# A mixture-of-experts layer: one TensorE signal for two steps of the shared expert, and the last batch's routing three steps sooner

## The chip, the core and the metric

The kernel runs on one core of a Trainium2 chip. The metric is the device time of one execution in microseconds (us), the median over several runs.

## The reference, cut to what matters

The input x has 8 batches of 512 rows of 128 numbers. An attention layer with 16 heads, a residual and a layer norm give x1. After it comes a mixture of experts: a gate picks two of eight experts for each row, and one shared expert takes every row.

```python
gates = sigmoid(xf @ Wg)
vals, idx = top_k(gates, 2); vals = vals / vals.sum(-1, keepdims=True)
shared = (silu(xf @ Ws1) * (xf @ Ws3)) @ Ws2
h = silu(einsum('td,edf->tef', xf, We1)) * einsum('td,edf->tef', xf, We3)
routed = einsum('tef,efd,te->td', h, We2, w)   # w: the two weights of each row, else 0
out = layernorm(x1 + (shared + routed) / 3)
```

## The kernel before

Every engine has its own program; they meet at semaphores only. There are three stages.

**Attention** runs quad by quad (four quads a batch, 32 in all) and works the routing of a batch into the attention of later ones. The routing of the last batch is left over, and parts of the last but one.

**The shared expert** has 32 steps, `n = 4 * b + c`: four for each batch b. Step (b, c) makes one 128 x 512 piece of the hidden layer, by three matmuls (lines 1477 to 1479) into bank c of `hT`. Even c is the half that goes through silu, odd c the half that it is multiplied with. So a pair of steps is worked off thus:

- ScalarE applies silu to the even bank (line 1367, `siluT_done`).
- VectorE multiplies it with the odd bank (line 1274, `gatedT_done`).
- TensorE may fill the pair's two banks again, one batch later, when that product is there (line 1475).

TensorE increments `hT_ready` after each step; ScalarE waits for `n + 1` at even n, VectorE at odd n.

Beside the steps run, in this order within a batch:

- At c = 0 TensorE turns the next batch's x1 (`turn_x`, line 679). ScalarE rounds it at c = 1 (`x_high`, line 686), VectorE takes the rest at c = 2 (`x_low`, line 691). Step (b + 1, 0) waits for both.
- At c = 1, 2, 3 TensorE does the second layer of the batch before (`shared_results`, line 1459), two tiles, one and one. It signals `ys_ready` after the last. Its first tiles wait for both products of that batch and for `sum_done`, which says that the results of the batch before that have been read out of the one bank they share.
- At c = 0 VectorE reads out those results, two batches back (`add_shared`, line 1262), in the order of its program: after the product of step (b, 3) and what stands beside that step.

What stands beside a step is written out by hand, by the step's number (`beside`, in TensorE's program for jobs, in VectorE's for routing). VectorE does the remaining routing of the last but one batch at steps 0 to 8, and that of the last at 9 to 25:

- `choose` pieces 0 to 7 at steps 9 to 16, one a step, each some two or three small instructions. They find each row's two experts.
- TensorE counts rows per expert (`count_rows`, at `COUNT_AT` = 16, after piece 6); VectorE reads the counts at step 17.
- `place` pieces 0 to 4 at steps 18 to 22. Piece 3 ends with `slot_i` (line 458), the slot of each row.
- The block owners at step 23, turned by TensorE at `OWNER_AT` = 24, read at 25 (`routed`).

When `slot_i` is there, GpSimd scatters the rows into their slots in DRAM by eight indirect DMAs (line 488). When they have all landed, SP's queue loads the blocks of 128 rows (line 1206).

**The routed experts**: TensorE does the last batch's `shared_results` (16 recorded matmuls), waits for `routed` and for the blocks and begins with 72 blocks (lines 1490, 1509 to 1532). For each, an indirect DMA from GpSimd writes the result to its rows (line 1178). Sums and the last layer norm run beside it.

Of the kernel before, what the change touches and what calls it, by code (L numbers as in the profile page):

```python
# [104 lines left out]
def layer(nc, x, w_qkv, b_qkv, w_out, b_out, wg, ws1, ws3, ws2, we1, we3, we2, out):  # L105
    B, S, D = x.shape
# [25 lines left out]
    with ctx:  # L132
        def sb(name, shape, dt=F32):
            return ctx.enter_context(nc.sbuf_tensor(name, shape, dt))
# [30 lines left out]
        ebT_low = sb("ebT_low", [P, 2, 512], F32R)  # L165
# [121 lines left out]
        def need(eng, s, value):  # L287

            if isinstance(value, int) and value <= 0:
                return  # L290
            eng.wait_ge(s, value)
            if not isinstance(value, int) and eng.engine in ALONE:


                eng.sem_inc(passed, 1)
# [374 lines left out]
        hT_ready = sem("hT_ready")  # L670
# [11 lines left out]
        def x_high(act, b):  # L682

            act.wait_ge(xT_ready, b + 1)
            need(act, hT_ready, 4 * (b - 1))
            act.activation(ebT_high[:, b % 2, :], xT_bank, ACT.Copy).then_inc(xT_high_done, 1)

        def x_low(dve, b):
# [378 lines left out]


        BESIDE = {0: ("counts", "valsT"), 1: ("oT",), 2: ("proj",), 7: ("x1T",), 8: ("gate",)}
        COUNT_AT, OWNER_AT = 16, 24  # L1070
        STAGE_OF = {"counts": 1, "valsT": 1, "oT": 1, "proj": 2, "x1T": 3, "gate": 3}

        early = prob[:, 0].rearrange("p h c t -> p (h c t)")
# [69 lines left out]
        hT = scoreA[:].rearrange("p a b x -> p (a b) x")  # L1143
# [71 lines left out]
        def moe_vector(dve):  # L1215
            def beside(n):

                if n == 0:
                    read_counts_job(dve, B)
                    dve_job(dve, "valsT", B, 1)  # L1220
                elif n in (1, 2):
                    place(dve, B - 2, n - 1)
                elif n == 3:
                    dve_job(dve, "proj", B, 2)
                    statistics(dve, B, 1)
                elif n == 4:
                    statistics(dve, B, 3)
                    statistics(dve, B, 5)
                elif n == 5:
                    place(dve, B - 2, 2)  # L1230
                elif n == 6:
                    normalize(dve, B, 1)
                    normalize(dve, B, 3)
                elif n in (7, 8):
                    place(dve, B - 2, n - 4)
                elif n == 9:
                    dve.wait_ge(job_read, jobs.number("gate", B, 3) + 1)
                    choose(dve, B - 1, 0)
                elif n in range(10, 17):
                    choose(dve, B - 1, n - 9)  # L1240
                elif n == 17:
                    dve.wait_ge(counts_ready, 1)
                    read_counts(dve, B - 1, shared, counts_read)
                    dve.wait_ge(counts_read, 1)
                elif n in range(18, 23):
                    place(dve, B - 1, n - 18)
                elif n == OWNER_AT - 1:

                    dve.wait_ge(late_const, 4)
                    dve.scalar_tensor_tensor(passed_ends[:], all_ends[:], block_no[:, 0:1], turn[:], ALU.is_le,  # L1250
                                             ALU.mult).then_inc(owner_done, 1)
                    dve.wait_ge(owner_done, 1)
                    dve.tensor_reduce(owner[:], passed_ends[:].rearrange("p b e -> p (b e)"), AX.X, ALU.add) \
                       .then_inc(owner_done, 1)
                elif n == OWNER_AT + 1:
                    dve.wait_ge(owner_ready, 1)
                    dve.tensor_copy(owner_i[0:1, :], late_owner).then_inc(routed, 1)
# [7 lines left out]
            for n in range(STEPS):  # L1265
                b, c = n // 4, n % 4
                if c == 0 and b >= 2:
                    add_shared(b - 2)
                if c % 2:

                    need(dve, ys_ready, b - 1)
                    dve.wait_ge(siluT_done, 2 * b + c // 2 + 1)
                    dve.wait_ge(hT_ready, n + 1)
                    dve.tensor_tensor(gatedT_shared[:, b % 2, c // 2, :], hT[:, c], silu_shared[:, c // 2, :],
                                      ALU.mult).then_inc(gatedT_done, 1)
                if c == 2 and b + 1 < B:
                    x_low(dve, b + 1)
                beside(n)
# [81 lines left out]
        def moe_scalar(act):  # L1360
            for n in range(STEPS):
                b, c = n // 4, n % 4
                if c % 2 == 0:
                    act.wait_ge(hT_ready, n + 1)

                    need(act, gatedT_done, 2 * (b - 1) + c // 2 + 1)
                    act.activation(silu_shared[:, c // 2, :], hT[:, c], ACT.Silu).then_inc(siluT_done, 1)
                if c == 1 and b + 1 < B:
                    x_high(act, b + 1)
                for kind in BESIDE.get(n, ()):  # L1370
                    if kind in ("oT", "x1T", "gate"):
                        act_job(act, kind, B, STAGE_OF[kind])

            def ebT_highs(r, n):
                act.wait_ge(ebT_ready, n + 1)
                need(act, h_ready, n - 1)
                act.activation(ebT_high[:, r % 2, 0:P], scoreA[:, 1, r % 2, 0:P], ACT.Copy).then_inc(ebT_high_done, 1)  # L1377

            ebT_highs(0, 0)
            ebT_highs(1, 1)  # L1380

            def final_normalize(batch, c):
                need(act, fmr_done, batch.n + 1)
                at = z[:, batch.slot, c, :]
                act.activation(at, at, ACT.Identity, scale=frs[:, c:c + 1], bias=fmr[:, c:c + 1]).then_inc(norm_done, 1)

            def store_out(batch):

                need(act, norm_done, 4 * (batch.n + 1))
                act.dma_start(out_rows[batch.n] if isinstance(batch.n, int) else  # L1390
                              out_rows[bass.ds(batch.n, 1)].rearrange("b p x -> (b p) x"),
                              z[:, batch.slot].rearrange("p c d -> p (c d)")).then_inc(out_stored[batch.slot], 16)

            NORMALIZED_AT = {4: (0,), 5: (1,), 6: (2, 3)}

            def block(g, r):
                k = g.k
                n = NBUF * k + r
                if exists(k, r):
                    act.wait_ge(h_ready, n + 1)  # L1400
                    need(act, gated_done, n - 1)
                    act.activation(silu[:, r % 2, :], scoreA[:, 0, r % 2, 0:F], ACT.Silu).then_inc(silu_done, 1)  # L1402
                if exists(k, r, 2):
                    c = (r - 2) % NBUF
                    at = NBUF * ((g.odd + (r - 2) // NBUF) % 2) + c
                    act.wait_ge(y_ready, n - 1)

                    need(act, y_stored[c], 16 * (k if r >= 2 else k - 1))
                    act.activation(yo[:, c, :], scoreB[:, r % 2, 0:D], ACT.Copy,  # L1409
                                   scale=eb[:, at, D + 1:D + 2]).then_inc(y_done, 1)  # L1410
                if exists(k, r, -2):
                    ebT_highs(r + 2, n + 2)
                if ended(g, 4):
                    for c in NORMALIZED_AT.get(r, ()):
                        final_normalize(ended(g, 4), c)
                    if r == NBUF - 1:
                        store_out(ended(g, 4))

            run_blocks(act, block)

        def moe_tensor(pe):
# [45 lines left out]
            for n in range(STEPS):  # L1467
                b, c = n // 4, n % 4

                at = E * 2 * F + (c % 2) * F + (c // 2) * P  # L1470
                high, low = (w[:, at:at + P] for w in w13_parts)
                if c == 0:
                    pe.wait_ge(xT_low_done, b + 1)

                need(pe, gatedT_done, 2 * (b - 1) + c // 2 + 1)

                pe.matmul(hT[:, c], high, ebT_high[:, b % 2, :], start=True, stop=False)
                pe.matmul(hT[:, c], low, ebT_high[:, b % 2, :], start=False, stop=False)
                pe.matmul(hT[:, c], high, ebT_low[:, b % 2, :], start=False, stop=True).then_inc(hT_ready, 1)
                if c == 0 and b + 1 < B:  # L1480
                    turn_x(pe, b + 1)
                if c and b:
                    shared_results(b - 1, ((0, 1), (2,), (3,))[c - 1])
                beside(n)
# [105 lines left out]
```

## Time and profile before, and how to read it

| what | us |
|---|---|
| time, median of 3 runs (lowest, highest) | 695.01 (694.5, 696.32) |
| span of the profiled execution | 737.1 |
| the profiled execution: TensorE busy | 656.4 |
| the profiled execution: VectorE busy | 551.6 |
| the profiled execution: ScalarE busy | 425.3 |
| the profiled execution: GpSimd busy | 269.0 |

The profiled execution is one that ran with the profiler on. Its span, from the first to the last instruction, is 42.1 us longer than the median time of the runs without it. Nothing else of that execution's time is recorded. Durations below are from it.

PE is TensorE, PEld its weight loads, DVE VectorE, ACT ScalarE, POOL GpSimd, SP SyncE, and a q behind a name that engine's queue or sequencer. L1479 is line 1479. A row's start is in us from the span's start; a number in brackets is how long the engine was idle before, and whom it waited for. Ends of matmuls are modelled, and an instruction of VectorE or ScalarE can begin before the row of the one before has ended. Tiles of the shared stage lie in the attention's `prob`, so many rows bear that name.

### The profile page before, as it was taken

To read this page: it belongs to the slowest core of one execution; us is meant where nothing else is said; L and a number is where in the kernel's file an instruction comes from. 1 tells how busy PE (TensorE), PEld (TensorE's weight loads), DVE (VectorE), ACT (ScalarE), POOL (GpSimd) and SP (SyncE) were. 2 spreads that over 40 slices of the span, in tenths; PEclk is the share of its full clock that TensorE was granted. 3 is DMA by queue.
4 is the path that set the end of the run, shared out by engine and by line. 5 is a ranking of instruction groups with operands and counts; after the bars stand their busy time and mean duration, and the time that the engine had idled before them with its cause. 6 is when DMAs were issued, how large, how long until landed. Compare 5 with 4: busy or idle time off the path is not lost.

```text
span 737.1 us, 16627 instructions
## 1 busy us (share of the span) xinstructions
PE 656.4 (89%) x4593; PEld 318.7 (43%) x4594; DVE 551.6 (75%) x1272; ACT 425.3 (58%) x973; POOL 269.0 (36%) x402
## 2 busy tenths in 40 slices
PE   2899999999899999999999999987988888888880
PEld 1232333333333343433433333322777766666660
DVE  4967777879779989998997997964756556666663
ACT  1056677677576677677676776673522344455442
POOL 3124114213154145134334334124144345555553
PEclk9999999999999999999999999998989999999885
DMA  4356766544234324333333333203111323433222
GB/s 79 75 130 153 145 136 120 110 89 92 57 66 97 82 61 91 70 80 79 71 76 84 74 55 85 53 24 113 38 44 40 78 76 99 123 113 110 89 71 71
DMA packets 161855, 62.65 MB, mean 85 GB/s; under 512 B 110586, under 2 KB 155516, under 8 KB 161808
## 3 DMA queue, kind: packets, MB, share of 16 engines
q1 hardware_dynamic: 155008, 46.72, 29.4%
q0 software_dynamic: 5648, 13.26, 6.0%
q10 hardware_dynamic: 1152, 2.10, 0.8%
q8 instruction: 23, 0.38, 0.2%
q14 instruction: 24, 0.20, 0.1%
HBM read 38.04 MB, written 24.26 MB: 85 GB/s over the span
## 4 chain that ended last, share of the span: by engine, by line
PE 76%; DVE 5%; issue 5%; ACT 4%; DMA 4%; another core or an unknown queue 2%; SPq 1%; POOL 1%; ACTq 0%; DVEq 0%; POOLq 0%
PE pvp L1018 16%; PE scoreB L998 15%; PE scoreA L984 14%; PE scoreB L1532 6%; PE scoreA L1509 3%; ACT prob L901 2%; PE scoreA L1511 2%; PE pvp L1519 2%; PE shared L525 2%; DMA parts_dram<-parts 2%; PE scoreA L1510 2%; DVE mx L928 2%; PE scoreB L1459 2%; PE shared L514 2%
## 5 line engine op out<-in xcount | busy, mean ns | idle before, releaser
L928 DVE TENSOR_REDUCE mx<-scoreA 128x2 f32<-128x1024 f32 x256 | 305.9, 1220 | 70.7 <-PE scoreA L984 68.3
L901 ACT ACTIVATE prob<-scoreB 128x512 f32<-128x512 f32 x512 | 279.5, 600 | 120.3 <-PE scoreB L998 117.9
L984 PE MATMUL scoreA<-ks,qs 72*128 72x512 bf16 x512 | 205.5, 409 | 14.8 <-DMA ks<-parts_dram 12.4
L998 PE MATMUL scoreB<-qs,ks 74*128 74x512 bf16 x512 | 200.5, 394 | 9.9 <-ACT prob L901 6.7
L1018 PE MATMUL pvp<-prob,v 128*32 128x512 f32 x1024 | 139.0, 616 | 0.8 <-ACT pv_sb L893 0.8
L984 PEld LDWEIGHTS scoreA<-ks,qs 72*128 72x128 bf16 x512 | 51.0, 102 | 155.6 <-DVE mx L928 66.7
L1178 POOL DMA_INDIRECT y_dram<-prob x72 | 70.7, 982 | 75.7 <-ACT prob L1409 50.5
L998 PEld LDWEIGHTS scoreB<-qs,ks 74*128 74x128 bf16 x512 | 49.8, 99 | 103.8 <-ACT prob L901 78.9
L488 POOL DMA_INDIRECT slots_dram<-rows,slot_i x64 | 63.3, 990 | 62.9 <-DMA ks<-parts_dram 31.2
L828 POOL CAST parts<-qk 128x256 bf16<-128x256 f32 x32 | 12.7, 397 | 187.2 <-ACT v_raw L563 168.4
L1409 ACT ACTIVATE prob<-scoreB,prob 128x128 f32<-128x128 f32 x72 | 26.5, 369 | 42.2 <-PE scoreB L1532 35.0
L1348 DVE TENSOR_TENSOR prob<-scoreA,prob 128x256 f32<-128x256 f32 x72 | 30.5, 423 | 22.5 <-ACT prob L1402 14.9
L1532 PE MATMUL scoreB<-w,prob 128*128 x288 | 47.3, 290 | 0.0
L1509 PE MATMUL scoreA<-w_high,ebT_high 128*128 x72 | 36.5, 508 | 11.1 <-DVE ebT_low L1283 6.8
L1402 ACT ACTIVATE prob<-scoreA 128x256 f32<-128x256 f32 x72 | 27.6, 384 | 29.6 <-PE scoreA L1511 19.8
L1283 DVE TENSOR_TENSOR ebT_low<-scoreA,ebT_high 128x128 fp32r<-128x128 f32 x72 | 20.7, 289 | 27.5 <-ACT ebT_high L1377 18.5
L1532 PEld LDWEIGHTS scoreB<-w,prob 128*128 128x128 f32 x288 | 40.5, 203 | 0.2
L1519 PE MATMUL pvp<-ident,prob 128*128 128x128 f32 x144 | 29.8, 290 | 10.9 <-DVE prob L1353 9.7
L1018 PEld LDWEIGHTS pvp<-prob,v 128*32 128x32 f32 x1024 | 20.5, 109 | 31.0 <-issue 29.5
L1353 DVE COPY prob<-pvp 128x256 f32<-128x256 f32 x72 | 29.9, 415 | 1.8 <-PE pvp L1519 1.8
L559 ACT ACTIVATE qk<-shared,bq 128x128 f32<-128x128 f32 x64 | 20.0, 363 | 18.4 <-PE shared L514 12.7
L1519 PEld LDWEIGHTS pvp<-ident,prob 128*128 128x128 f32 x144 | 16.7, 146 | 30.0 <-issue 16.0
(172 smaller groups left out, 886.5 us busy)
## 6 DMA issues: line engine op xcount, KB each, us to landing
qs<-parts_dram SPq DMA_DIRECT2D x96, 96.0 KB
parts_dram<-parts SPq DMA_DIRECT2D x32, 192.0 KB
slots_dram<-blank POOLq DMA_DIRECT2D x9, 520.0 KB
prob<-slots_dram SPq DMA_DIRECT2D x72, 65.0 KB
ks<-parts_dram SPq DMA_DIRECT2D x64, 64.0 KB
prob<-y_dram SPq DMA_DIRECT2D x8, 512.0 KB
ks<-parts_dram SPq DMA_DIRECT2D x32, 96.0 KB
xin<-in_L_attn_x SPq DMA_DIRECT2D x32, 64.0 KB, 2.3
```

The costliest lines, as they stand in the source:

```text
L488: pool.indirect_dma_start(slots_dram, bass.IndirectOffsetOnAxis(ap=slot_i[:, j, t:t + 1], axis=0), rows[:, t, j, :], None).then_inc(scatte ...
L901: act.activation(prob[:, i % 2, j, 2 * u + c, :], scoreB[:, c], ACT.Exp, scale=SCALE).then_inc(exp_done, 1)
L928: dve.tensor_reduce(mx[:, i % 2, at // 2, at % 2 * 2:at % 2 * 2 + 2], scoreA[:, at % 2], AX.X, ALU.max).then_inc(max_done, 1)
L984: ins = pe.matmul(scoreA[:, at % 2, c], qs[0:KR, st, j, qc * P:(qc + 1) * P], ks[0:KR, st, j, :], start=True, stop=True)
L998: pe.matmul(scoreB[:, c], ks[0:KM, i, j, kc * P:(kc + 1) * P], qs[0:KM, i, j, :], start=True, stop=True).then_inc(b_ready, 1)
L1018: ins = pe.matmul(pvp[32 * h:32 * h + 32, :], v[:, (i - 1) % 2, h, j, :], prob[:, (i - 1) % 2, h, j, :], start=(j == 0), stop=(j == 3))
L1178: pool.indirect_dma_start(y2_dram, bass.IndirectOffsetOnAxis(ap=eb[:, at, D:D + 1].bitcast(I32), axis=0), yo[:, r, :], None, bounds_check= ...
L1348: dve.tensor_tensor(gated[:, r % 2, :], scoreA[:, 0, r % 2, F:2 * F], silu[:, r % 2, :], ALU.mult) \
L1353: dve.tensor_copy(gatedT[:, (r - 1) % 2, :], pvp[:, 0:F]).then_inc(gT_copied, 1)
L1509: pe.matmul(h, ebT_high[:, r % 2, 0:P], high, start=True, stop=False)
L1519: ins = pe.transpose(pvp[:, c * P:(c + 1) * P], gated[:, (r - 1) % 2, c * P:(c + 1) * P], ident[:])
L1532: ins = pe.matmul(y, gatedT[:, r % 2, c * P:(c + 1) * P], w2_flat[:, bass.ds(e * NFC * D + c * D, D)], start=(c == 0), stop=(c == NFC - 1))
```

## The change

Four things change.

- TensorE increments `hT_ready` at odd c only. ScalarE's silu of an even step and VectorE's product wait for `n // 2 + 1`, so both for the end of the pair's odd step. `x_high`'s bound is halved to match.
- VectorE's choice for the last batch goes two pieces a step: 0 and 1 at step 9, then 2 and 3, 4 and 5, 6 and 7 at steps 10 to 12.
- The counts go from step 16 to 13 (read at 14 instead of 17), the five pieces of `place` from 18 to 22 to 15 to 19.
- The owners go from steps 23, 24 and 25 to 20, 21 and 22.

```diff
-            need(act, hT_ready, 4 * (b - 1))
+            need(act, hT_ready, 2 * (b - 1))
...
-        COUNT_AT, OWNER_AT = 16, 24
+        COUNT_AT, OWNER_AT = 13, 21
...
                 elif n == 9:
                     dve.wait_ge(job_read, jobs.number("gate", B, 3) + 1)
                     choose(dve, B - 1, 0)
-                elif n in range(10, 17):
-                    choose(dve, B - 1, n - 9)
-                elif n == 17:
+                    choose(dve, B - 1, 1)
+                elif n in range(10, 13):
+                    choose(dve, B - 1, 2 * (n - 9))
+                    choose(dve, B - 1, 2 * (n - 9) + 1)
+                elif n == 14:
                     dve.wait_ge(counts_ready, 1)
                     read_counts(dve, B - 1, shared, counts_read)
                     dve.wait_ge(counts_read, 1)
-                elif n in range(18, 23):
-                    place(dve, B - 1, n - 18)
+                elif n in range(15, 20):
+                    place(dve, B - 1, n - 15)
...
-                    dve.wait_ge(hT_ready, n + 1)
+                    dve.wait_ge(hT_ready, n // 2 + 1)
...
-                    act.wait_ge(hT_ready, n + 1)
+                    act.wait_ge(hT_ready, n // 2 + 1)
...
-                pe.matmul(hT[:, c], high, ebT_low[:, b % 2, :], start=False, stop=True).then_inc(hT_ready, 1)
+                ins = pe.matmul(hT[:, c], high, ebT_low[:, b % 2, :], start=False, stop=True)
+                if c % 2:
+                    ins.then_inc(hT_ready, 1)
```

## Rows read from the trace of the kernel before

**Rows 1.** The page: the chain that ended last, and one group of DMAs.

```profile
PE 76%; DVE 5%; issue 5%; ACT 4%; DMA 4%; another core or an unknown queue 2%; SPq 1%; POOL 1%; ACTq 0%; DVEq 0%; POOLq 0%
...
xin<-in_L_attn_x SPq DMA_DIRECT2D x32, 64.0 KB, 2.3
```

**Rows 2.** TensorE's groups, 517 to 575 us: busy us, mean ns, idle us before.

```profile
L1459 PE MATMUL scoreB<-w,prob 128*128 128x128 f32 x128 | 19.0, 286 | 2.7 <-DVE prob L1262 2.7
L1477 PE MATMUL scoreA<-ebT_high,w_high 128*128 128x512 f32 x32 | 15.7, 491 | 2.5 <-DVE prob L1274 2.5
...
L538 PE MATMUL shared<-ident,x 128*128 128x128 f32 x4 | 0.6, 279 | 0.7 <-DVE x L628 0.7
```

**Rows 3.** The chain that ended last, 530 to 640 us: start, us, what.

```profile
544.60 0.61 ACT prob L1367
545.28 0.69 DVE prob L1274
...
552.94 0.23 PE scoreA L1479
...
554.31 0.44 PE scoreB L679 x4
...
555.45 0.89 PE scoreB L1459 x8
```

**Rows 4.** VectorE in stretches holding one piece each: stretch, us, busy, clock, DMA.

```profile
534.24:534.88 0.64, 0.58 (x3) 1.00 0.33 104
...
543.07:543.38 0.31, 0.28 (x3) 1.00 0.00 0
543.99:544.40 0.41, 0.37 (x3) 1.00 0.00 0
550.71:551.67 0.96, 0.89 (x7) 0.50 0.00 0
532.16:532.80 0.64, 0.61 (x7) 1.00 0.39 102
```

**Rows 5.** Timeline of VectorE, around step 19.

```profile
553.31 0.69 DVE L1274 TENSOR_TENSOR prob<-scoreA,prob 128x512 f32<-128x512 f32 x1 [1.64 <-PE scoreA L1479]
553.92 0.17 DVE L426 TENSOR_TENSOR_SCAN ends<-ones,more 128x8 f32<-128x8 f32 x1
```

**Rows 6.** Timeline of VectorE, the product of step 3.

```profile
524.60 0.69 DVE L1274 TENSOR_TENSOR prob<-scoreA,prob 128x512 f32<-128x512 f32 x1 [0.59 <-PE scoreA L1479]
```

**Rows 7.** Timeline from the slots to the end of the shared stage.

```profile
557.15 0.17 DVE L458 CAST slot_i<-slot 128x8 int32<-128x8 f32 x1
...
568.85 8.66 SPq L1206 DMA_DIRECT2D prob<-slots_dram  x16
...
569.69 0.40 PE L1479 MATMUL scoreA<-ebT_low,w_high 128*128 128x512 f32 x1
...
570.22 0.69 DVE L1274 TENSOR_TENSOR prob<-scoreA,prob 128x512 f32<-128x512 f32 x1 [0.27 <-PE scoreA L1479]
...
571.66 2.02 PE L1459 MATMUL scoreB<-w,prob 128*128 128x128 f32 x16 [1.13 <-DVE prob L1262]
```

**Rows 8.** Timeline of steps 13 to 16, while GpSimd issues indirect DMAs.

```profile
538.09 0.40 PE L1479 MATMUL scoreA<-ebT_low,w_high 128*128 128x512 f32 x1
...
542.47 0.69 DVE L1274 TENSOR_TENSOR prob<-scoreA,prob 128x512 f32<-128x512 f32 x1 [4.10 <-PE scoreA L1479]
...
544.13 0.50 PE L1477 MATMUL scoreA<-ebT_high,w_high 128*128 128x512 f32 x1 [2.48 <-DVE prob L1274]
```

**Rows 9.** Stretches of 10 us: engines' busy us, granted clock, DMA share, GB/s.

```profile
540.00:550.00 10.00, 6.80 (x33) 5.64 (x32) 4.78 (x16) 2.33 (x4) 3.75 (x7) 0.76 0.07 22
550.00:560.00 10.00, 9.76 (x57) 8.30 (x56) 7.94 (x36) 2.93 (x6) 2.02 (x2) 0.90 0.02 7
```

**Rows 10.** L1509 (one a block) in two stretches of the routed stage.

```profile
577.02:580.08 3.06, 0.96 (x2) 0.39 (x3) 1.00 0.34 75
585.47:591.02 5.55, 1.44 (x3) 0.56 (x3) 1.00 0.23 66
```

## The prediction, made before the changed kernel was run

> **What bounds the kernel now.** I read the chain that ended last first: TensorE carries 76% of the span and VectorE 5% [rows 1]. So a change beside TensorE counts only where TensorE waits for it. Next, TensorE's groups over the shared stage, the only stage the change touches: it waits 2.7 us before the second layer, for `add_shared`; 2.5 us before a step's first matmul, for a product; and 0.7 us before x1's transposes [rows 2]. Everything else there runs without idle time. In particular no idle time is booked between a signalling matmul and the next instruction, so dropping sixteen increments frees no time on TensorE itself. Then the timelines, for the distance between a step's end and each of those waits; and last the stretches, for clock and lateness (below).
>
> **One signal for two steps: what a product costs in time.** Before, silu of the even step ran while TensorE was still in the odd step, and the product began 0.14 us after the odd step's end: step 19 ended at 552.94 + 0.23 = 553.17, its product began at 553.31 [rows 3, 5]; for step 31 it is 570.09 and 570.22 [rows 7]. Now silu itself waits for the odd step. From the odd step's end: 0.03 us to ScalarE (an estimate, somewhat under VectorE's 0.14), silu 0.60, and 0.07 from silu to product (544.60 + 0.61 to 545.28) [rows 3]. Together 0.70 us, so every product comes 0.56 us later. That is certain, 16 times; what matters is where TensorE has less slack than that.
>
> The bound is the chain from step (b, 3) through `add_shared` to the second layer at step (b + 1, 1). VectorE is held 0.61 us by the product (553.31 to 553.92) [rows 5], then does what stands beside the step (call it p), then `add_shared`, 0.68 us like the other 512-wide operations, and TensorE follows 0.15 us after it (the second layer at 571.66, when an `add_shared` started as soon as the product of 570.22 let go) [rows 7]. Before: 0.14 + 0.61 + 0.68 + 0.15 = 1.58 + p. After: 2.14 + p. TensorE gets there 2.28 us after the step's end (553.17 to 555.45) [rows 3], as step, turn, step and the last second-layer tiles lie between. So before there was 0.70 us of room for p; after there is 0.14, and the rest of p is idle time on TensorE. This is where the two halves of the change meet: the doubled choice makes p larger just when the room goes.
>
> Term by term, with pieces from [rows 4]:
> - Step 11: p is choice pieces 4 and 5, 0.31 + 0.41 = 0.72 us (before, one piece). Wait 0.58. VectorE is also behind: from the product of step 9 it does 0.61, pieces 0 and 1 (0.64 + some 0.4), x_low 0.6 and pieces 2 and 3 (some 0.8), 3.05 us, starting 0.70 after step 9's end. It is free at 3.75; the product of step 11 is due 2.73 (0.89 + 0.70 + 0.44 + 0.70) + 0.70 = 3.43 after that end. 0.3 more: **0.9**.
> - Step 15: p is `place` piece 0, 0.96: **0.8**.
> - Step 19: p is piece 4, 0.64: **0.5**.
> - Step 27: p is 0, but the last batch has no turn in between (0.44 less [rows 3]): 1.84 against 2.14, **0.3**.
> - Step 31: TensorE waits 1.13 us before the last second layer already [rows 7], so the later product is paid in full: **0.55**.
> - The first batches: x1's transposes wait for a VectorE that has no pause from step 1's product to the normalize but 0.59 us before step 3's [rows 6]. Step 1's product slips 0.56, step 3's by that again, less the pause, plus TensorE's own slip through the attention output's later copy on ScalarE (which now stands behind a later silu). Bounds 0.55 and 1.2; taken **1.0**.
>
> Sum 4.05, taken as 4.0 us. If all slips were hidden it would be 0; with the upper bound at each place (each p with its semaphore gaps, 0.1 to 0.2 more) 5.5.
>
> **Counts, placing, owners three steps sooner.** Same instructions, none added; their room beside the steps is counted in p. On TensorE the count and the owners' transpose only change place: nothing, or up to 0.7 us less if a wait of the count for the choice goes. The slots are ready three steps sooner, some 3 to 4 us. GpSimd has nothing queued before the scatter by then and SP nothing but the block loads, so both start sooner. What is that worth? From `slot_i` at 557.15 eight scatters run until SP issues the first load at 568.85; with the 2.3 us that a 64 KB load takes to land [rows 1] block 0 is there at about 571.2, while TensorE is busy until 573.68 [rows 7]. So the blocks are 2.5 us early already, and earlier still buys nothing. If TensorE's two late waits are taken out (below), it arrives at about 571.3, a tie: still nothing. The cover for the later start is gone only if TensorE came faster.
>
> **Late signals.** One thing in the trace speaks for the change. Step 13 ended at 538.49, yet its product began at 542.47, VectorE idle for 4.1 us, and TensorE then stood 2.48 us [rows 8] and fell to 1.2 GHz for parts of the next stretches (clock 0.76 and 0.90) [rows 9]. ScalarE's silu at 544.60 [rows 3] is as late. This happens only while GpSimd issues indirect DMAs. It happens in the routed stage too: blocks come every 1.53 us at first, then every 1.85 us [rows 10], 0.32 us x 72 = 23 us. With fewer signals, fewer could be late.
>
> How does the profiled execution stand to the runs? It is 42.1 us longer than the median. The 23 us, some 7.5 us in the shared stage (2.48, 1.6 of the 2.7, and 3.4 for the clock: 0.24 and 0.10 of 10 us) and the clock's loss in the routed stage make up most of those 42. So I take it that timed runs have few late signals, and the sum of 4.0 holds for them: 695.0 + 4.0 = **699.0 us** (the profiled execution: 737.1 to 741).
>
> **Rivals.**
> 1. *Late signals are real in timed runs; the halved number ends them.* TensorE sends four instead of six signals a batch (two pairs, the turn, the second layer). All 7.5 us back, less the 4.0: 3.5 us faster, 691.5. It decides for faster once over 6.1 us of 7.5 come back. For: [rows 8, 9]. Against: the 42 us, and that a pair's signal can be late as well, with less room behind it. The Trainium skill, "VectorE: DVE Perf Modes", section on the TRN2 errata, warns that dense increments on completion from several engines should be spaced; by that rule this change is the remedy and the time would go down; the trace agrees that signals arrive late, not why. Chance 0.13.
> 2. *The routing's tail binds in timed runs.* If scatter and load take 2 to 4 us longer without the profiler's company than [rows 7] show, or late signals cost half of theirs, what the earlier slots return cancels the later products: 694.5 to 697. For: the tie above. Against: nothing shows such a load. Chance 0.2.
> 3. *The slips are hidden.* If ScalarE and VectorE hand over faster than in the rows, 0.56 shrinks and the room of 0.14 grows; only the end's 0.55 and part of the first batch remain, 696. This goes into rival 2's chance.
>
> The forecast, slower by 2.1 to 6 us, has 0.67. 0.3% of 695 us is 2.1 us, about what a measurement of this kernel can tell from no change. Faster 0.13, same 0.2, slower 0.67. The range reaches down through the same case and up to 5.5 us and a little, for a lost clock: 694.3 to 701.0. The forecast's own range is 697.2 to 701.0.
>
> **What would show it.** Right: silu of each even step starts after the odd L1479's end; TensorE's idle time before L1459 grows from 2.7 us, spread over steps 13, 17, 21 and 29, and that before L538 from 0.7 to about 1.7; L458 comes some 14 us or more before TensorE reaches L1490, which waits for no block. Wrong: no idle time before L1459 outside the last one; or, for rival 1, products that begin within 0.2 us of silu all through the scatters, with the clock at full between; or L1490 waiting for blocks in the old kernel.

## The result, and the profile after

The changed kernel takes 702.88 us (median of 6 runs, 700.99 to 706.49), the kernel before in the same session 694.75 us (6 runs, 691.88 to 696.32): ratio 1.0133, 95% interval 1.0105 to 1.016. A second timing gave 1.0106, 1.007 to 1.0143. So it is slower, by some 8 us; 4 were forecast, in a range up to 701.0 us. The profiled execution took 703.39 us, with a span of 701.6.

The profile of before that the prediction read was of an unusual execution: its span of 737.1 us and its late signals [rows 8, 10] came back in none of the later profiles. A second profile of the unchanged kernel has a span of 694.0 us, in a run of 695.73. It is called **before 2** here, and everything below is measured against it.

TensorE's groups from 505 to 575 us: busy us, mean ns, idle us before them. First before 2, the undisturbed form of [rows 2]:

```profile
L1459 PE MATMUL scoreB<-w,prob 128*128 128x128 f32 x128 | 18.0, 276 | 1.2 <-DVE prob L1262 1.1
L1477 PE MATMUL scoreA<-ebT_high,w_high 128*128 128x512 f32 x32 | 15.1, 472 | 0.0
...
L538 PE MATMUL shared<-ident,x 128*128 128x128 f32 x4 | 0.6, 280 | 0.7 <-DVE x L628 0.7
```

Then the changed kernel, whose lines here lie two further on (L1461 is L1459, L1479 is L1477, L1264 is L1262; L538 and L691 are unmoved):

```profile
L1461 PE MATMUL scoreB<-w,prob 128*128 128x128 f32 x128 | 18.3, 278 | 4.1 <-DVE prob L1264 4.1
L1479 PE MATMUL scoreA<-ebT_high,w_high 128*128 128x512 f32 x32 | 15.2, 474 | 2.4 <-DVE ebT_low L691 2.4
...
L538 PE MATMUL shared<-ident,x 128*128 128x128 f32 x4 | 0.6, 279 | 1.2 <-DVE x L628 1.2
```

Three things can be read off. The wait before the second layer grew by 2.9 us, about as the prediction said, and the one before x1's transposes (L538) by 0.5, half of what it said. But a step's first matmul, which waited for nothing, now waits 2.4 us, and not for a product: for `x_low` (L691). No term of the prediction stands for that.

The timeline of TensorE in the changed kernel gives the places:

```profile
526.64 0.63 PE L538 MATMUL shared<-ident,x 128*128 128x128 f32 x4 [1.21 <-DVE x L628]
...
533.84 0.50 PE L1479 MATMUL scoreA<-ebT_high,w_high 128*128 128x512 f32 x1 [0.68 <-DVE ebT_low L691]
...
536.82 1.13 PE L1461 MATMUL scoreB<-w,prob 128*128 128x128 f32 x8 [0.89 <-DVE prob L1264]
...
542.41 0.51 PE L1479 MATMUL scoreA<-ebT_high,w_high 128*128 128x512 f32 x1 [1.74 <-DVE ebT_low L691]
...
545.03 1.13 PE L1461 MATMUL scoreB<-w,prob 128*128 128x128 f32 x8 [0.51 <-DVE prob L1264]
...
550.91 1.13 PE L1461 MATMUL scoreB<-w,prob 128*128 128x128 f32 x8 [0.64 <-DVE prob L1264]
...
561.27 1.13 PE L1461 MATMUL scoreB<-w,prob 128*128 128x128 f32 x8 [0.33 <-DVE prob L1264]
...
566.39 2.02 PE L1461 MATMUL scoreB<-w,prob 128*128 128x128 f32 x16 [1.72 <-DVE prob L1264]
```

The second layers are those of steps 13, 17, 21 and 29 and the last, just the places named; the two L1479 are steps 12 and 16.

Outside the shared stage nothing changed that the profiles show. The attention stage before it ends at 513.28 us in the changed kernel and at 512.90 in before 2 (from 508.2 to 515.6 in the twelve later profiles, a scatter that the shared stage does not have). The 72 blocks' first matmuls start from 569.5 to 678.9 us in the changed kernel and from 561.8 to 671.1 in before 2, 109.4 and 109.3 us; in the first profile, that of [rows 10], it was 137.4. Nor is the clock a part of it. Stretches of the changed kernel, as in [rows 9]:

```profile
540.00:550.00 10.00, 7.75 (x47) 6.24 (x46) 8.10 (x36) 2.28 (x4) 2.90 (x6) 1.00 0.01 3
550.00:560.00 10.00, 9.36 (x60) 7.99 (x59) 5.27 (x12) 3.37 (x6) 6.43 (x7) 1.00 0.16 52
```

The granted clock is 1.00 in both, 2.4 GHz. So the **shared stage** is the measure from here on: from the start of step 0's first matmul to that of the first block's. It is 561.83 - 512.90 = 48.93 us in before 2 and 569.50 - 513.28 = 56.22 in the changed kernel, 7.29 us longer; a second profile of it gives 7.08. The timed losses, 7 and 9 us by the two ratios, agree with that within their intervals.

### The profile page after: what moved, and what is told of

The parts are those of the page before. It is cut to its first block, busy times and chain, and to the rows that moved or that the text cites. A ratio compares the mean times of both kernels' runs of the same rounds, so it can differ in the third digit from the quotient of the medians.

```text
span 701.6 us, 16626 instructions
## 1 busy us (share of the span) xinstructions
PE 642.9 (92%) x4593; PEld 307.9 (44%) x4594; DVE 551.2 (79%) x1272; ACT 426.2 (61%) x973; POOL 269.5 (38%) x402
## 4 chain that ended last, share of the span: by engine, by line
PE 70%; DMA 7%; DVE 7%; ACT 4%; issue 4%; SPq 4%; POOL 2%; ACTq 0%; DVEq 0%; POOLq 0%
PE pvp L1018 16%; PE scoreB L998 15%; PE scoreA L984 14%; DMA parts_dram<-parts 5%; PE scoreB L1536 4%; PE pvp L1523 3%; DVE mx L928 2%; ACT prob L901 2%; PE scoreA L1513 2%; PE scoreA L1515 2%; PE scoreA L1514 2%; PE shared L525 2%; DMA ks<-parts_dram 2%; PE shared L514 1%; SPq L764 1%
## 5 line engine op out<-in xcount | busy, mean ns | idle before, releaser
L1536 PE MATMUL scoreB<-w,prob 128*128 x288 | 44.4, 277 | 0.1
L1536 PEld LDWEIGHTS scoreB<-w,prob 128*128 128x128 f32 x288 | 37.8, 191 | 0.5 <-issue 0.3
L1513 PE MATMUL scoreA<-w_high,ebT_high 128*128 x72 | 34.4, 478 | 0.9 <-DVE ebT_low L1285 0.9
L636 POOL TENSOR_SCALAR veps<-mv 128x4 f32<-128x4 f32 x8 | 1.8, 228 | 75.7 <-DVE mv L618 75.7
L1515 PE MATMUL scoreA<-w_high,ebT_low 128*128 x72 | 28.6, 397 | 0.0
```

The source lines that it names most:

```text
L1513: pe.matmul(h, ebT_high[:, r % 2, 0:P], high, start=True, stop=False)
L1515: pe.matmul(h, ebT_low[:, r % 2, 0:P], high, start=False, stop=True).then_inc(h_ready, 1)
L1536: ins = pe.matmul(y, gatedT[:, r % 2, c * P:(c + 1) * P], w2_flat[:, bass.ds(e * NFC * D + c * D, D)], start=(c == 0), stop=(c == NFC - 1))
```

## The experiments

The table gives, for each kernel, how many us later than in before 2 a step's first matmul starts, counted from that of step 0 (from the timelines' starts, to 0.01 us or so). The column heads are steps; "blocks" is the first block's first matmul. A difference between two columns is what was lost in between. The last column is the timed ratio.

| kernel | 8 | 12 | 14 | 16 | 18 | 22 | 25 | 30 | blocks | ratio (95% interval) |
|---|---|---|---|---|---|---|---|---|---|---|
| changed | 0.85 | 1.76 | 3.36 | 5.35 | 5.70 | 6.42 | 6.01 | 6.70 | 7.29 | 1.0133 (1.0105, 1.016) |
| changed, again | 0.85 | 1.78 | 3.38 | 5.14 | 5.49 | 6.22 | 5.81 | 6.49 | 7.08 | 1.0106 (1.007, 1.0143) |
| single signal only | 0.85 | 1.44 | 2.47 | 2.48 | 3.38 | 3.70 | 4.10 | 4.67 | 5.26 | 1.0061 (1.0036, 1.0087) |
| sooner routing only | 0.02 | 0.02 | 0.99 | 4.29 | 5.47 | 5.72 | 5.31 | 5.30 | 5.30 | 1.0077 (1.0039, 1.0115) |
| changed, spare tile | 0.86 | 1.79 | 3.39 | 3.39 | 4.36 | 5.02 | 4.61 | 5.30 | 5.89 | 1.0081 (1.0051, 1.0112) |
| the same, again | 0.86 | 1.78 | 3.38 | 3.38 | 4.17 | 4.83 | 4.42 | 5.11 | 5.70 | 1.0098 (1.0069, 1.0127) |
| sooner routing, spare tile | 0.00 | -0.01 | 0.98 | 0.98 | 0.97 | 1.58 | 1.17 | 1.17 | 1.17 | 1.0014 (0.9981, 1.0046) |
| single signal but for step 8 | 0.83 | 0.82 | 1.27 | 1.27 | 1.83 | 2.15 | 2.56 | 3.12 | 3.71 | 1.0043 (1.0008, 1.0077) |
| three signals a step | 0.00 | 0.00 | 0.00 | 0.00 | 0.00 | -0.16 | -0.16 | -0.16 | -0.16 | 1.0005 (0.9967, 1.0043) |
| end bank | 0.00 | -0.01 | -0.01 | -0.01 | -0.01 | -0.15 | -0.15 | -0.16 | -0.82 | 0.9985 (0.9958, 1.0012) |
| end bank, sooner, spare | 0.00 | 0.00 | 0.97 | 0.98 | 0.97 | 1.64 | 1.23 | 1.23 | 0.56 | 1.0005 (0.9978, 1.0033) |

**Before 2.** The kernel before, unchanged, profiled a second time.

> The kernel before, unchanged, for a second profile of it. If the late TensorE signals of the first profile (span 737.1 us) are not part of the timed runs, as I took it, the span is about 693 us, products start within 0.2 us of silu all through the scatters, and the shared stage takes about 47 us from the first step's matmul to the last second-layer matmul. If they belong to the kernel, the span is again over 730 us and the stage about 56 us.

Measured: span 694.0 us, stage 48.93 us against 574.77 - 517.62 = 57.15 in the first profile, no late signals. The prediction's reading of the 42.1 us as late signals that timed runs don't have was right; rival 1 lost what it stood on.

**Single signal only.** The change without the sooner routing.

```diff
-        COUNT_AT, OWNER_AT = 13, 21
+        COUNT_AT, OWNER_AT = 16, 24
...
-                    choose(dve, B - 1, 1)
-                elif n in range(10, 13):
-                    choose(dve, B - 1, 2 * (n - 9))
-                    choose(dve, B - 1, 2 * (n - 9) + 1)
-                elif n == 14:
+                elif n in range(10, 17):
+                    choose(dve, B - 1, n - 9)
+                elif n == 17:
```

> One signal for two steps, the routing where it was. Theory 1 (the guard): the signals cost only what the later products cost, 1.0 at x1's transposes, 0.3 at step 11, 0.2 at 15, 0.3 each at 19, 23 and 27, 0.55 at the end, in all some 2.9 us: about 697.7, ratio 1.004. Theory 2 (all of the loss is later products): 6 to 9 us, ratio 1.009 to 1.013. If fewer signals help: under 1.000.

Measured: 699.22 us, ratio 1.0061, stage 5.26 us longer. That lies between the two theories. So the later products alone cost more than the whole sum forecast, and the choice, one piece a step here, is not what makes them dear. 0.90 us of it is a wait of the count at step 16 for a later piece 6 (between the table's steps 16 and 18), and 0.40 one for the owners; these two are gone where the routing comes sooner.

**Sooner routing only.** The change with a signal at every step.

```diff
-                ins = pe.matmul(hT[:, c], high, ebT_low[:, b % 2, :], start=False, stop=True)
-                if c % 2:
-                    ins.then_inc(hT_ready, 1)
+                pe.matmul(hT[:, c], high, ebT_low[:, b % 2, :], start=False, stop=True).then_inc(hT_ready, 1)
```

> The choice, counts, placing and owners three steps sooner, with a signal for each step. Theory 1 (the guard: piece 7 overwrites the row weights and so waits until the scatter of the batch before has landed, with VectorE's whole program behind it): VectorE idles 3 us or more before L374, TensorE 2 us or more before step 16, and the kernel is 4 to 6 us slower, ratio 1.006 to 1.009. Theory 2 (larger pieces beside the steps, the guard hidden): at most 1 us slower, ratio up to 1.002.

Measured: 700.09 us, ratio 1.0077, stage 5.30 us longer. So the half that was costed at nothing is as dear as the other, and 3.30 of its 5.30 are lost between steps 14 and 16. Timeline rows of VectorE and of TensorE in this kernel, and one stretch:

```profile
538.82 0.17 DVE L374 SCALAR_TENSOR_TENSOR rows<-top,tot 128x8 f32<-128x8 f32 x1 [4.97 <-DMA slots_dram<-rows,slot_i]
...
540.29 0.80 PE L1479 MATMUL scoreA<-ebT_high,w_high 128*128 128x512 f32 x1 [3.05 <-DVE ebT_low L691]
...
540.00:550.00 10.00, 9.54 (x49) 8.04 (x50) 8.71 (x39) 2.88 (x5) 2.59 (x6) 0.83 0.02 7
```

VectorE stands 4.97 us in the last piece of the choice. Line 374 writes the last batch's two weights into `rows`, the tile out of which GpSimd is still scattering the batch before, and line 373 waits until that scatter has landed. The product of step 13 and `x_low` for step 16 are queued behind it, and TensorE stands 3.05 us. After that the clock was granted at half, 1.2 GHz, for 3.4 us (0.83 over the stretch of 10 us: 0.17 x 10 / 0.5). In those 3.4 us lie steps 16 and 17, which lose 1.2 us more. Theory 1 had forecast both waits and the ratio.

The same rows in the changed kernel, VectorE's and GpSimd's:

```profile
537.11 0.18 DVE L371 RECIPROCAL tot<-tot 128x4 f32<-128x4 f32 x1
540.93 0.17 DVE L374 SCALAR_TENSOR_TENSOR rows<-top,tot 128x8 f32<-128x8 f32 x1 [3.65 <-DMA slots_dram<-rows,slot_i]
541.07 0.69 DVE L1276 TENSOR_TENSOR prob<-scoreA,prob 128x512 f32<-128x512 f32 x1
541.68 0.68 DVE L691 TENSOR_TENSOR ebT_low<-scoreB,ebT_high 128x512 fp32r<-128x512 f32 x1
...
538.36 0.96 POOL L488 DMA_INDIRECT slots_dram<-rows,slot_i  x1 [0.30 <-issue]
540.97 1.17 POOL L477 COPY rows<-x 128x512 f32<-128x512 f32 x2 [1.65 <-DMA slots_dram<-rows,slot_i]
```

The last of the eight scatters is issued at 538.36 and has landed by 540.93, 2.6 us later; VectorE, the product and `x_low` follow at once. And in before 2:

```profile
538.35 0.18 DVE L371 RECIPROCAL tot<-tot 128x4 f32<-128x4 f32 x1
...
539.65 0.17 DVE L374 SCALAR_TENSOR_TENSOR rows<-top,tot 128x8 f32<-128x8 f32 x1 [1.13 <-DMA slots_dram<-rows,slot_i]
539.79 0.69 DVE L1274 TENSOR_TENSOR prob<-scoreA,prob 128x512 f32<-128x512 f32 x1
```

Piece 7 at step 16 met the landing with 1.13 us of waiting, and little of that seems to have reached TensorE: in the profiles of "three signals" and "end bank", with the same routing, the wait was 0.96 and 0.99 us, and step 22 started 0.16 and 0.15 us sooner. So already there the choice ended against that wait; the change moved it four steps sooner.

**Changed, with a spare tile.** The last batch's weights go into a tile of their own, `w_late`; GpSimd copies them into `rows` later, and the wait moves to where `slot_i` is written. It was timed twice.

```diff
-                need(dve, scattered, CLEARED + 16 * NCH * TOP_K * b)
-                dve.scalar_tensor_tensor(rows[:, :, :, D + 1].rearrange("p t j -> p j t"), top[:],
+                last = isinstance(b, int) and b == B - 1
+                if not last:
+                    need(dve, scattered, CLEARED + 16 * NCH * TOP_K * b)
+                to = w_late[:] if last else rows[:, :, :, D + 1].rearrange("p t j -> p j t")
+                dve.scalar_tensor_tensor(to, top[:],
...
+            pool.tensor_copy(rows[:, :, :, D + 1], w_late[:].rearrange("p j t -> p t j")).then_inc(rows_done, 1)
```

> The changed kernel, but the last batch's weights go to a spare tile, so that piece 7 waits for no scatter; GpSimd copies them into the rows after it has copied those, and the wait for the earlier scatter stands before slot_i is written. Theory 1 (the guard): VectorE's idle 3.65 us before L374 goes, and with it some 4 to 5 us: about 699, ratio 1.005 to 1.007, the 4.0 us of my sum left. Theory 2: still 8 us or more slower, ratio 1.011 or more, the idle time turning up elsewhere on VectorE.

> A second timing of the change with the spare tile for the last batch's weights, in which the choice's last piece waits for no scatter. Theory, the wait for the scatter is a part of the change's loss: a ratio of 1.007 to 1.010, under the changed kernel's 1.0106 to 1.0133, and a shared stage of 54.5 to 55.2 us. Rival, the first timing was low by chance and the wait only takes the place of other idle time: a ratio of 1.011 to 1.013, though the profile's stage is again shorter than 56 us.

Measured: 1.0081 and 1.0098, stages 5.89 and 5.70 us longer instead of 7.29 and 7.08. So some 1.4 us come back, not the 4 to 5 of the first expectation. Step 16 loses nothing now, where it lost 1.99 and 1.76; step 18 loses 0.97 and 0.79 where it had lost 0.35, so a part comes back. (A little of that is something else: with the wait gone, GpSimd copies the rows just then, and VectorE's first instruction of `place` beside it takes 0.51 and 0.32 us in these two profiles, 0.21 in the changed kernel.) The wait is worth 1.2 to 1.6 us of the changed kernel's stage. The intervals of the ratios overlap, so the times by themselves do not show it; the four profiles do.

**Changed, again.** A second timing and a second profile.

> The changed kernel again, for a narrower interval and a second profile. By steps, its shared stage came out 7.3 us longer than that of the second profile of the kernel before (56.22 against 48.93 us to the first block). If nothing outside that stage is slower, the ratio is 1.0105, 702.0; if another stage loses as well, 1.013 or more. The stage again within 0.3 us of 56.2.

Measured: 702.76 us, ratio 1.0106, stage 56.01 us. So its first profile was no odd execution; the loss and its places are the same.

**Sooner routing with the spare tile**, a signal at every step: the two edits above together.

> Routing three steps sooner, a signal for each step, and the spare tile, so that no piece of the choice waits for the earlier scatter. Theory 1 (guard): of the 5.3 us that the sooner routing alone cost the shared stage, only the wait at step 13 is left, 0.4 us, and the stage takes 49 to 49.6 us: ratio 0.999 to 1.002. Theory 2 (VectorE too full with two pieces a step): 2 us or more stay, ratio 1.003 or more.

Measured: 695.32 us, ratio 1.0014, stage 1.17 us longer, where 0.1 to 0.7 was expected. Of the 5.30 us of the sooner routing 4.13 hang on that wait, its lost clock with it. What is left comes before three second layers, TensorE's waits in this kernel (`add_shared` is L1273 here):

```profile
536.16 1.13 PE L1470 MATMUL scoreB<-w,prob 128*128 128x128 f32 x8 [0.31 <-DVE prob L1273]
...
542.03 1.13 PE L1470 MATMUL scoreB<-w,prob 128*128 128x128 f32 x8 [0.19 <-DVE prob L1273]
...
547.79 1.13 PE L1470 MATMUL scoreB<-w,prob 128*128 128x128 f32 x8 [0.53 <-DVE prob L1273]
```

Beside step 15 that is p, now too large for the room that the prediction worked out (0.70 us), even without later products. At steps 11 and 19 VectorE, still at the pieces before, also comes to the product itself 0.25 us later than in before 2.

**Single signal but for step 8.** Silu of step 8 is let go by step 8 itself, as before; all other pairs have one signal. The idea: on ScalarE the last gate of the attention stands behind that silu.

```diff
+        def signals(n):
+            return (n + 1) // 2 + (1 if n >= 8 else 0)
...
-                    act.wait_ge(hT_ready, n // 2 + 1)
+                    act.wait_ge(hT_ready, 5 if n == 8 else signals(n | 1))
...
-                if c % 2:
+                if c % 2 or n == 8:
                     ins.then_inc(hT_ready, 1)
```

> One signal for two steps but for step 8, which signals by itself. Beside step 8 stands the gate's exponential, for which ScalarE loads another table (1.28 us) and back. Theory 1 (silu of step 8, when it waits for step 9, pushes the table load, the gate and x's rounding behind it): the wait of 0.6 us before step 12 goes, and the one at step 13 shrinks from 1.0 to 0.4 us or less; the stage 1.2 us or more shorter than with all pairs (54.2), about 53, ratio 1.003 to 1.005. Theory 2 (the table load stays hidden, only the 0.56 us of the later product count): at most 0.6 us shorter.

Measured: 698.26 us, ratio 1.0043, stage 3.71 us longer instead of 5.26. Steps 12 and 14 together lose 0.44 instead of 1.62. The chain, on ScalarE and VectorE in the changed kernel:

```profile
530.03 0.60 ACT L1369 ACTIVATE prob<-scoreA 128x512 f32<-128x512 f32 x1 [2.12 <-PE scoreA L1481]
530.64 1.28 ACT L573 ACT_TABLE_LOAD   x1
531.94 0.20 ACT L573 ACTIVATE ge<-shared 128x32 f32<-128x32 f32 x1
532.03 0.59 ACT L686 ACTIVATE ebT_high<-scoreB 128x512 fp32r<-128x512 f32 x1
532.64 1.28 ACT L1369 ACT_TABLE_LOAD   x1
533.93 0.60 ACT L1369 ACTIVATE prob<-scoreA 128x512 f32<-128x512 f32 x1
...
532.16 0.18 DVE L330 TENSOR_SCALAR tmp<-ge 128x32 f32<-128x32 f32 x1 [0.65 <-ACT ge L573]
533.10 0.68 DVE L691 TENSOR_TENSOR ebT_low<-scoreB,ebT_high 128x512 fp32r<-128x512 f32 x1
```

and in before 2:

```profile
526.78 0.60 ACT L1367 ACTIVATE prob<-scoreA 128x512 f32<-128x512 f32 x1
527.40 1.28 ACT L573 ACT_TABLE_LOAD   x1
```

Silu of step 8 now waits 2.12 us for step 9. The gate's table load and the gate are queued behind it, the choice's first piece (L330) waits for the gate, and `x_low` of step 12 stands behind that piece and, in the changed kernel, behind the second one too. The load of silu's table and silu of step 10 come later as well, and with them the product of step 11. (The Trainium skill, "ScalarE: Activation LUTs", section "What ACT_TABLE_LOAD costs", has 1283 ns for the load, which the rows show, and 1380 ns of draining besides, which they do not: the silu ends at 530.63 and the gate starts at 531.94.)

**Three signals a step.** The kernel before, whose other two matmuls of a step also increment a semaphore that nobody reads: 96 increments instead of 32.

```diff
+        spare = sem("spare")
...
-                pe.matmul(hT[:, c], high, ebT_high[:, b % 2, :], start=True, stop=False)
-                pe.matmul(hT[:, c], low, ebT_high[:, b % 2, :], start=False, stop=False)
+                pe.matmul(hT[:, c], high, ebT_high[:, b % 2, :], start=True, stop=False).then_inc(spare, 1)
+                pe.matmul(hT[:, c], low, ebT_high[:, b % 2, :], start=False, stop=False).then_inc(spare, 1)
```

> The kernel before, with every step's first and second matmul also incrementing a semaphore that nobody reads: 96 increments in place of 32. If an increment costs TensorE nothing, as no idle time after a signalling matmul suggests, the shared stage stays at 48.9 us to 0.1 and the ratio is 0.998 to 1.002. If increments cost or hold each other up, 64 more show: 0.05 us each would be 3 us, ratio 1.004 or more, or products that begin late.

Measured: 695.68 us, ratio 1.0005 (0.9967, 1.0043), stage 0.16 us shorter. Increments cost nothing that can be seen, and 64 more made no signal late. (The 0.16 us fit the shorter wait of piece 7 there, above.) The note that the prediction took from the Trainium skill, "VectorE: DVE Perf Modes", section on the TRN2 errata, asks to space dense increments because of a deadlock and names no cost in time; none shows in this run.

**End bank**, and the same with the sooner routing and the spare tile: what might beat the kernel before. The last second layer goes into the bank in which x1 was turned.

```diff
-                    need(pe, sum_done, b)
+                    if b < B - 1:
+                        need(pe, sum_done, b)
+                to = xT_bank if b == B - 1 else ys_bank
...
-                        ins = pe.matmul(ys_bank[:, t * P:(t + 1) * P],
+                        ins = pe.matmul(to[:, t * P:(t + 1) * P],
```

> The kernel before, with one thing else: the last batch's second layer goes into the bank that the turned x1 had, which nobody reads any more by then, so it doesn't wait for the results of the batch before to be read out (before, unchanged: 1.13 us of idle time ahead of its last L1459 x16). If that wait is time on the path, the shared stage, 48.93 us from the first step's first matmul to the first block's, becomes 47.7 to 48.0, and the time about 1 us shorter, a ratio of 0.998 to 1.000. Rival: the blocks aren't there yet; the first block's turn (L1490) then waits instead, and the stage stays within 0.3 us of 48.9. By the earlier view that no block is late (the prediction's), the gain is whole.

> The same edit together with the sooner routing and the spare tile for the weights (signal after each step). There the slots are ready sooner, so no block can be late: the stage goes from 50.1 to 49.0 us by its profile. If the blocks bind in the kernel above, this one gains more from the edit (1.1 us) than that one does; if they don't, both gain 1.1 us and this one stays 1.2 us longer. Ratio 0.998 to 1.001 by the first theory's sum; under 0.997 only if the sooner slots are worth something in timed runs that the profiles don't show.

Measured: 0.9985 and 1.0005; the stage's end gains 0.66 us in the one and 0.67 in the other. TensorE's end in the first of them:

```profile
560.55 2.05 PE L1461 MATMUL scoreB<-w,prob 128*128 128x128 f32 x16 [0.44 <-DVE prob L1274]
562.43 0.67 PE L1492 MATMUL scoreA<-ident,prob 128*128 128x128 f32 x2
```

The wait shrinks from 1.13 to 0.44 us and is then one for the last product: that is the miss of both expectations, which had 1.1. No wait is booked before the blocks' turn, and the kernel with the sooner slots gains no more, so no block is late. Neither kernel can be told from the kernel before by its time.

## Why the forecast was half of the loss

Term by term, the stage of the changed kernel against the prediction's sum:

| what | predicted | measured | lost before step |
|---|---|---|---|
| the first batches | 1.0 | 0.85 | 3, 8 |
| step 12: `x_low` behind the gate's chain | not named | 0.91 | 12 |
| second layer of step 13 (the gate's chain has a part in it) | 0.9 | 1.19 | 14 |
| step 16: piece 7's wait for the scatter | not named | 1.99 | 16 |
| second layer of step 17 (the scatter's wait has a part in it) | 0.8 | 0.76 | 18 |
| second layer of step 21 | 0.5 | 0.72 | 22 |
| the owners' transpose gone from step 24, with its wait | 0 | -0.41 | 25 |
| not assigned | | 0.13 | 26 |
| second layer of step 29 | 0.3 | 0.56 | 30 |
| the end | 0.55 | 0.59 | blocks |
| sum | 4.05 | 7.29 | |

(Step 14 lost 1.60, of which 0.41 is the count that moved there and is got back at step 17. Of the 0.72 of step 21 some 0.08 is the owners' transpose, which moved there.) The six terms of the prediction came to 4.67 for 4.05. **The mechanism of the single signal was right** where nothing else held VectorE, at step 21, at step 29 and at the end. Rival 3 is out with that: the products did come later. The hand-off, as the chain of waits of the changed kernel has it (compare [rows 3, 5]):

```profile
558.88 0.25 PE scoreA L1481
...
559.15 0.61 ACT prob L1369
...
559.83 0.69 DVE prob L1276
560.52 0.61 DVE prob L1264
...
561.27 0.35 PE scoreB L1461
```

From the step's end, 559.13, the product is 0.70 us away, as worked out, and the second layer 2.14. The terms were a little small since a wait costs more than its booked idle time: step 30 starts 0.56 us later for 0.33 of idle time, step 12 0.91 for 0.68. In the rows a matmul starts some 0.17 us before the one ahead of it has ended, and a wait ends that overlap; and the eight matmuls of a second layer take 1.13 us after a wait, 1.05 without one.

**At steps 13 and 17 the right size was in part luck.** The three products before the second layers of steps 13, 17 and 21, in the changed kernel:

```profile
534.62 0.69 DVE L1276 TENSOR_TENSOR prob<-scoreA,prob 128x512 f32<-128x512 f32 x1
...
542.71 0.69 DVE L1276 TENSOR_TENSOR prob<-scoreA,prob 128x512 f32<-128x512 f32 x1
...
548.73 0.69 DVE L1276 TENSOR_TENSOR prob<-scoreA,prob 128x512 f32<-128x512 f32 x1 [0.66 <-ACT prob L1369]
```

Only the third waits for silu, as the chain of the prediction has it. The first comes just behind the late silu of step 10 and VectorE's pieces; the second finds VectorE busy without a pause since the scatter landed at 540.93. Without the scatter's wait, in the kernel with the spare tile, step 17's second layer costs 1.41 and 1.22 us (from step 17 to step 18) instead of the 0.8 forecast.

**The step that failed** is "Same instructions, none added; their room beside the steps is counted in p". It costs the moved pieces by their durations and names no wait in them. It asks what GpSimd has queued only for the scatter after the slots, not for the earlier scatter that still runs when the moved pieces come up. Piece 7 has a wait in it (line 373) for GpSimd's scatter of the batch before. At step 16 that was nearly over; moved to step 12, VectorE stands there, with a product and `x_low` behind it: 1.99 us. The first profile could have told. GpSimd's next use of `rows` there follows the scatter's landing, at 544.25, and piece 7 at 547.21 did not wait,

```profile
544.25 1.17 POOL L477 COPY rows<-x 128x512 f32<-128x512 f32 x2 [1.45 <-DMA slots_dram<-rows,slot_i]
...
547.21 0.17 DVE L374 SCALAR_TENSOR_TENSOR rows<-top,tot 128x8 f32<-128x8 f32 x1
```

but only because the late signal had held VectorE 4.1 us [rows 8] before that piece came up. Its price could have been estimated from these rows: the several us between the moved piece and 544.25. The second step that failed is in the term of the first batches, for the silu of step 8: it followed the later silu to the attention output's copy, but not to the gate and its table load, which stand behind it too: 0.91 us before step 12 and a part of step 14. Together the two unnamed waits are 2.9 of the 3.2 us that the sum lacked, by the table. By the runs, the scatter's wait is worth 1.4 us (7.29 less 5.89, 7.08 less 5.70) and the gate's chain 1.55 us, this in the kernel with the single signal alone (5.26 less 3.71). No run takes out both, so that their sum holds in the changed kernel is not shown. One reading of the rows was wrong too, at no cost to the sum: that everything else in the stage ran without idle time. The view of [rows 2] also has 0.7 us before the count (L494), 0.5 before L525 and 0.2 before the owners' transpose (L1449).

The halves do not add up: 5.26 and 5.30 apart, 7.29 together. When the products are later, VectorE reaches the scatter's wait later and stands there less (TensorE loses 1.99 instead of 3.30 and keeps its clock), and the waits for the count (before step 17, with the single signal alone) and for the owners go when these come sooner.

Rival 2 fell too: the sooner slots bring nothing, since no block was late. In the changed kernel they are not even sooner: `slot_i` comes 547.90 - 513.28 = 34.62 us after the stage's start, in before 2 546.06 - 512.90 = 33.16, three steps sooner but in steps that start some 5.7 us later.

## What to carry to other kernels

When work is moved to an earlier step, go through its waits one by one: for each, say when what it waits for is done, and whether that was met early or just in time at the old place; a row with no wait there may be a wait that something else was hiding. When an instruction is made to wait longer, follow everything behind it in its engine's program to the next one that the bound engine needs, table loads and other stages' work among it. And take a second profile before working from one whose span does not agree with its runs: here the odd one hid the wait that decided.

## What the runs showed of the hardware that was not expected

- TensorE's signals were some 4 us late in one profiled execution (a step ended at 538.49, its product began at 542.47 [rows 8]), whose span was 42 us over the median, and in none of the twelve profiles taken afterwards of this kernel and its variants. What caused them stays open; the count of increments did not bring them back (96 instead of 32).
- After standing for 3.05 us TensorE was granted 1.2 GHz for 3.4 us in the kernel with the sooner routing only; after 1.74 us in the changed kernel it kept 2.4 GHz. In the first profile it fell after 2.48 us [rows 8, 9].
- The change of ScalarE's table costs 1.31 us from the end of one activation to the start of the next, 1.28 of it the load.
- A new wait of TensorE cost 0.23 to 0.25 us more than its booked idle time: 0.33 booked cost 0.56, 0.51 cost 0.76, 0.68 cost 0.91 and 1.74 cost 1.99 (changed kernel).
